# Layer 1's products as 8 bases x 16 features, with one and two picks by turns, in a two-layer graph network on one Trainium2 core

## What is computed

```python
x = _layernorm(x + L0(x, ...))
h = x
xs, y = h[src], h[dst]
c = w_comp[etype]
xb = einsum('ei,bio->ebo', xs, weight)
msg = einsum('eb,ebo->eo', c, xb)
x_hat = xs @ A1_w.T + A1_b
y_hat = y @ A2_w.T + A2_b + rel_emb[etype]
a = tanh(relu(sum(x_hat * y_hat, -1) / sqrt(32)))
nei = segment_sum(a[:, None] * msg, dst)
h_new = where(in_deg > 0, nei + h[src[last_e]] @ self_loop_weight, 0)
out = _layernorm(x + relu(h_new))
```

## Time and profile before

| | |
|---|---|
| median of 3 runs | 4324.56 us |
| profiled execution / its span | 4323.87 / 4322.1 us |
| TensorE busy, VectorE busy | 3720.5 us (86%), 2847.5 us (66%) |
| POOL busy, ACT busy | 3200.7 us (74%), 741.1 us (17%) |
| granted TensorE clock, mean over the span | 0.950 |
| DMA traffic | 649.66 MB, mean 150 GB/s |
| layer 1's first and last `x4_load` | 2215.7 and 4137.2 us |

### The profile page before, as it was taken

How to read it: one execution, slowest core, us unless ns; L and a number is a source line. 1 busy time by engine, 2 the same in 40 slices (tenths; PEclk the granted TensorE clock), 3 DMA queues, 4 the chain that set the end, 5 groups by cost and what they waited for, 6 DMA issues and landing times.

```text
span 4322.1 us, 58432 instructions
## 1 busy us (share of the span) xinstructions
PE 3720.5 (86%) x20607; PEld 1663.8 (38%) x20607; DVE 2847.5 (66%) x5125; ACT 741.1 (17%) x1303; POOL 3200.7 (74%) x3330
## 2 busy tenths in 40 slices
PE   7989999999999999941788999989999899989841
PEld 3444554554554544421333333333333333333311
DVE  8845555555555555526668888888888888888844
ACT  4411111111111111110011111111111111111111
POOL 7777777777777777767777777777777777777745
PEclk9999999999999999965899999999999999999965
DMA  8146566666666666651146666666666666666621
GB/s 340 26 109 169 148 160 148 157 160 151 156 159 152 158 156 152 159 138 33 29 104 182 176 174 168 180 174 172 170 177 175 175 171 173 176 176 169 168 60 32
DMA packets 546562, 649.66 MB, mean 150 GB/s; under 512 B 219555, under 2 KB 381888, under 8 KB 544096
## 3 DMA queue, kind: packets, MB, share of 16 engines
q1 hardware_dynamic: 394912, 480.58, 42.4%
q0 software_dynamic: 106432, 56.28, 8.3%
q10 hardware_dynamic: 44928, 109.07, 6.5%
HBM read 421.88 MB, written 223.66 MB: 149 GB/s over the span
## 4 chain that ended last, share of the span: by engine, by line
PE 54%; DMA 12%; DVE 11%; POOL 7%; issue 5%; SPq 1%; ACT 1%; DVEq 0%; POOLq 0%; ACTq 0%
PE psum L1488 23%; PE psum L1524 6%; DMA late<-xs_dram 6%; PE psum L1646 5%; DVE late L1322 5%; POOL rows_in L760 4%; DMA xs_dram<-rows_in 4%; PE psum L1573 4%; PE psum L1582 3%; PE psum L1726 3%; PE psum L1534 2%; POOL last_rows L760 2%; PE psum L1474 2%; DVE dt_ L1206 2%; DMA rows_in<-h_dram,src_idx 2%
## 5 line engine op out<-in xcount | busy, mean ns | idle before, releaser
L760 POOL DMA_INDIRECT rows_in<-h_dram,src_idx x1540 | 1453.4, 944 | 476.0 <-issue 410.0
L760 POOL DMA_INDIRECT rows_in<-in_x_dram,src_idx x1392 | 1353.6, 972 | 434.6 <-issue 418.0
L1322 DVE TENSOR_TENSOR late<-late,psum 128x512 f32<-128x512 f32 x1664 | 1082.9, 681 | 359.3 <-PE psum L1573 192.0
L1488 PE MATMUL psum<-early,late 128*128 128x448 bf16 x5712 | 1130.6, 353 | 7.1 <-DVE late L1118 5.0
L1488 PEld LDWEIGHTS psum<-early,late 128*128 128x128 bf16 x5712 | 544.8, 98 | 625.3 <-issue 137.4
L1573 PE MATMUL psum<-comp,sel 128*128 128x512 bf16 x1664 | 573.7, 385 | 168.4 <-DVE late L1322 167.1
L1582 PE MATMUL psum<-late,basis 128*32 128x512 f32 x3328 | 446.7, 609 | 0.0
L1118 DVE TENSOR_TENSOR late<-psum,lane_hot 128x448 f32<-128x448 f32 x272 | 169.9, 625 | 358.7 <-PE psum L1488 270.8
L1646 PE MATMUL psum<-x,rows_in 128*128 128x448 bf16 x1344 | 381.0, 353 | 0.0
L1573 PEld LDWEIGHTS psum<-comp,sel 128*128 128x128 bf16 x1664 | 155.5, 98 | 574.9 <-DVE late L1322 460.0
L1234 DVE TENSOR_TENSOR_SCAN scan<-fresh,scan,psum 128x512 f32<-128x512 bf16 x103 | 131.8, 1280 | 352.9 <-PE psum L1534 352.9
(11 more groups left out here) (157 smaller groups left out, 4149.8 us busy)
## 6 DMA issues: line engine op xcount, KB each, us to landing
late<-xs_dram SPq DMA_DIRECT2D x416, 256.0 KB
sp_in<-spread SPq DMA_DIRECT2D x208, 256.0 KB
late<-type_dram SPq DMA_DIRECT2D x104, 512.0 KB, 9.2
onehot_dram<-late SPq DMA_DIRECT2D x104, 512.0 KB
late<-onehot_dram SPq DMA_DIRECT2D x104, 512.0 KB
sum_rows<-early ACTq DMA_DIRECT2D x104, 512.0 KB, 2.7
spread<-late SPq DMA_DIRECT2D x16, 1664.0 KB, 40.1
ea<-in_edge_t SPq DMA_DIRECT2D x104, 256.0 KB
```

The costliest lines, as they stand in the source:

```text
L760: pool.indirect_dma_start(out=out, out_offset=None, in_=table, in_offset=bass.IndirectOffsetOnAxis(ap=index, axis=0)).then_inc(done, 16)
L1322: dve.tensor_tensor(prod[:, n % G_BUFS, :], x4[:, s.slot(2), g, :], bank[C_BANK[n]][:, :], ALU.mult).then_inc(prod_ready, 1)
L1488: last_ = pe.matmul(hot_bank[tile_slot(s, t)], class_hot[s.slot(2)][:, c, HOT - hot_tiles(s) + t, :], x_parts[:, c, q, :], start=c == 0 an ...
```

## The change

Three things change, nearly all of them in layer 1.

1. A product holds 8 bases x 16 features on its partitions, in place of 4 x 32. A coefficient tile then serves both halves of the 32 features: there are 8 coefficient tiles (2 groups of bases j, 4 streams g) and 8 double products of 128x1024, whose coefficient operand is the PSUM bank read twice (a broadcast over the two halves i). The 16 message matmuls of a step stay as they are in number and shape.
2. The source rows must now stand as 8 copies of 16 features x 2 halves: `x8` takes 2 MB a step, and `x8_load` is eight DMAs, the k-th onto partitions 16k to 16k+15, in runs of 2 KB as before.
3. `HOTS1` is (1, 2): even steps of 6 to 98 pick one tile, odd ones two (46 steps pick one tile more, so POOL issues 46 gathers fewer). The second tile uses PSUM bank 1, between the copies of `compose` and `score_sum`. `PIECES1` is written anew, and so is the order of `step1` on TensorE and VectorE. In layer 0 `hot_save` stores two tiles for the odd steps.

The diff, cut to its core (the views and index tables that only follow from the sizes are left out):

```diff
+B_GROUPS = 2
+F_GROUPS = KCH // B_GROUPS
+OPS = B_GROUPS * STREAMS
+COPIES = BASES // B_GROUPS
+FEATS = F // F_GROUPS
...
-HOTS1 = (1,)
-PIECES1 = {1: (0, 0, 6, 11, 11, 16, 21)}
+HOTS1 = (1, 2)
+PIECES1 = {1: (0, 0, 5, 12, 21), 2: (0, 7, 16, 28, 42)}
...
-C_BANK = [(2, 3, 6)[n % 3] for n in range(SLOTS - 1)] + [3]
+C_BANK = [(2, 3, 6)[n % 3] for n in range(OPS)]
...
-        hot_bank1 = [bank[5][:, 0:PICK * F]]
+        hot_bank1 = [bank[b][:, 0:PICK * F] for b in (1, 5)]
...
-                n = max(HOTS1)
+                n = max(hot1_count(s.at), 1)
...
-                wait_step(sp, s, prod_ready, each=SLOTS, lag=2)
-                for k in range(4):
-                    sp.dma_start(x4[F * k:F * k + F, u, :, :], xs_dram[u].rearrange("(g f) n -> f g n", f=F)
-                                 ).then_inc(x4_in[u], 16)
+                wait_step(sp, s, prod_ready, each=OPS, lag=2)
+                for k in range(COPIES):
+                    sp.dma_start(x8[FEATS * k:FEATS * k + FEATS, u].rearrange("p g i n -> p (g i) n"),
+                                 xs_dram[u].rearrange("(m f) n -> f m n", f=FEATS)
+                                 ).then_inc(x8_in[u], 16)
...
-                dve.tensor_tensor(prod[:, n % G_BUFS, :], x4[:, s.slot(2), g, :],
-                                  bank[C_BANK[n]][:, :], ALU.mult).then_inc(prod_ready, 1)
+                dve.tensor_tensor(prods[n], x8[:, s.slot(2), g],
+                                  bc(bank[C_BANK[n]][:, :], [P, F_GROUPS, LEN], 1), ALU.mult).then_inc(prod_ready, 1)
...
+                if hot1_count(s.at + 1) == len(hot_bank1):
+                    wait_count(pe, s, hot1_read, hot1_before(s.at + 1) + 1)
                 pe.matmul(bank[1][:, :], ones_blk[:, :], score, start=True, stop=True).then_inc(sum_done, 1)
...
-                    if rest == 0:
+                    if rest == 0 and t < hot1_count(s.at) - 1:
+                        wait_step(pe, s, comp_ready, each=2, lag=1)
+                    elif rest == 0:
                         wait_step(pe, s, query_ready, lag=1)
```

More of the change, by code:

```diff
@@ L66 @@
 CLASS_COLS = HOT_COLS + EARLY_TILES
-C_BANK = [(2, 3, 6)[n % 3] for n in range(SLOTS - 1)] + [3]
-C_FREE = [max(m for m in range(-SLOTS, n) if C_BANK[m % SLOTS] == C_BANK[n]) + 1 for n in range(SLOTS)]
-G_BUFS = 8
+C_BANK = [(2, 3, 6)[n % 3] for n in range(OPS)]
+C_FREE = [max(m for m in range(-OPS, n) if C_BANK[m % OPS] == C_BANK[n]) + 1 for n in range(OPS)]
+LATE_PRODS = 4
 BURST = 4
@@ L319, in build @@
         out1 = [out1_all[:, (u + 1) % 4] for u in range(4)]
+        y_room = early[:, NODE_COLS * F:NODE_COLS * F + 2 * F_GROUPS * LEN]
+        prods = [room[:, a:a + F_GROUPS * LEN].rearrange("p (i n) -> p i n", i=F_GROUPS)
+                 for room, n in ((late_prods, LATE_PRODS), (ea[:, :, :].rearrange("p u n -> p (u n)"), 1),
+                                 (out0[:, :, :, :].rearrange("p u k f -> p (u k f)"), 1), (y_room, 2))
+                 for a in range(0, n * F_GROUPS * LEN, F_GROUPS * LEN)]
         at[0] = 0
@@ L447, in build @@
         xs_out = [sem(f"xs_out{u}") for u in range(2)]
-        x4_in = [sem(f"x4_in{u}") for u in range(2)]
+        x8_in = [sem(f"x8_in{u}") for u in range(2)]
         hot_in = sem("hot_in")
@@ L1668, in step1 @@
                 if behind.exists():
-                    messages(behind, KCH - 1)
-                coef(s, 3)
+                    messages(behind, 2)
+                    messages(behind, 3)
                 if more:
                     compose(ahead)
-                coef(s, 4)
+                coef(s, 3)
                 if more:
@@ L1676, in step1 @@
                     spread_turn(1, ahead, 4)
-                coef(s, 5)
-                if more:
                     relate(ahead)
-                coefs(s, 6, 8)
+                coef(s, 4)
+                if pick:
+                    hot_rows(later, 0)
                 if turn:
                     source_turn(ahead)
[L1683 to L1688, removed]
+                coef(s, 5)
                 if pick:
                     hot_rows(later, 1)
-                coef(s, 11)
-                coef(s, 12)
+                messages(s, 0)
+                coef(s, 6)
+                messages(s, 1)
                 if more and not turns_last:
@@ L1698, in step1 @@
                     hot_rows(later, 2)
-                coef(s, 13)
+                coef(s, 7)
                 if pick:
                     hot_rows(later, 3)
[L1702 to L1708, removed]
                 if behind.exists():
@@ L1789 @@
         w2[o:o + HID, q, F * (g % 2):F * (g % 2) + F] = np.asarray(L0_gnn_W2)
-    sel = np.zeros((2, 64, 2, KCH, 4, F), f32)
+    sel = np.zeros((2, 64, 2, B_GROUPS, COPIES, FEATS), f32)
     for half in range(2):
         for q in range(PARTS):
-            for k in range(KCH):
-                for b in range(4):
-                    sel[half, q * BASES + 4 * k + b, half, k, b, :] = 1.0
+            for j in range(B_GROUPS):
+                for b in range(COPIES):
+                    sel[half, q * BASES + COPIES * j + b, half, j, b, :] = 1.0
     rel = np.zeros((P, F + BASES), f32)
```

67 lines of the change are left out of this document (34 added, 33 removed).

## The result

The changed kernel takes a median of 5617.98 us (5605.07 to 5641.34, 4 runs) against 4323.41 us (4322.13 to 4326.15, 4 runs): 1.3001 times as long, 95% interval 1.298 to 1.3023. Its profiled execution took 5623.68 us, of which the span is 5621.9 us. The prediction was 4637 us and its range ended at 5131; the serial load, one of its rivals, stood at 5667.

The account below looks back on a forecast made before the run. POOL's gathers were taken to bound layer 1, with the ring 2.3 us behind. A round of 16.36 + 0.15 + 5.1 = 21.6 us over 101 steps adds 302.9, other loads 10.2: 4323.9 + 313 = 4637 us, range 4265 to 5131.

Parts of the forecast that it names:

- the serial load: Rival: the eight copy DMAs go one after the other at 104 GB/s, a round of 31.6 us, 5667 us; chance 0.14.
- POOL is the bound: Layer 1 before the change: 15 gathers of 1.248 us make the 18.7 us step.
- the ring: Layer 1's loop of load, product 0, turn, store and load, once per step: 16.36 us a round before the change.
- 2.3 us of room: Layer 1: POOL's 18.67 us step less the 16.36 us loop; all that the new load may cost.
- the 57.4 us: POOL in layer 1: 46 gathers fewer at 1.248 us each, gained only while POOL is the bound.
- slower, 0.86: Whole kernel: chance of a slower time, from 0.72 for the forecast and 0.14 for the serial load.
- The load's rate: Load of the spread rows, 2.10 MB in eight DMAs: 207 GB/s assumed, 10.1 us, so +5.1 us a round.
- The path from product 0 to the turn: Layer 1, on the ring: 3.96 us before, 4.5 with two picks or 3.7 with one after, +0.15 us in the mean.
- The store's 3.9 us stay: Store of the turned source rows, on the ring: unchanged at 3.9 us.
- 21.6: Forecast length in us of one round of the ring after the change: 16.36 + 0.15 + 5.1.
- VectorE nothing, TensorE nothing: Layer 1 busy time: VectorE stays 15.2 us a step, TensorE 17.1 in the mean, below POOL's 18.1; no cost.
- hidden load: Rival: copies load at 390 GB/s, the ring is 16.8 us, POOL stays the bound, 4267 us; chance 0.11.

Follow-up runs that it names:

- e1: Changed kernel with copy k of the source rows written to every eighth partition, `sel` and `basis` permuted to match; 4766.81 us (1.1022 to the kernel before).
- e15: Changed kernel with spread copies issued by SP and ScalarE, small loads ahead of them, and the next step's source-row turn directly behind `compose`; 4332.6 us (1.0008).
- e16: e15 with the step before's two messages put back ahead of the turn, one into each of TensorE's two waits; 4277.29 us (0.989).
- e11: Changed kernel with the early turn alone: next step's source rows turned ahead of the coefficient that product 0 sets free; 5391.93 us (1.2457).
- e2: Changed kernel with SP issuing copies 0 to 3 and ScalarE copies 4 to 7, partitions still neighbouring; 5042.55 us (1.166).
- e3: Changed kernel with the edits of both e1 and e2: spread partitions and two issuing engines; 4668.73 us (1.08).

## Why the prediction was wrong

- **POOL is the bound, the ring runs close behind with 2.3 us of room, and the load decides**: right. The ring became the bound and the 57.4 us won nothing. The direction (slower, 0.86) was right.
- **The load's rate: the step that failed.** "I take the rate of the nearest row, 207 GB/s", because "if some engines get ahead and work on the next DMA, two narrow ones do together what one wide one did". They did not: 119 to 128 GB/s, and 21.7 us from first issue to product 0 (mean of 22.14 and 21.17) where 7.16 + 5.1 = 12.3 were forecast. That is +9.4 us a round. With the same bytes on every eighth partition the rate came (206 to 212 GB/s in e1), so what the step had wrong is that neighbouring 16-partition DMAs in one queue help each other along. The argument against it stood in the text, that four different old DMAs in flight had got no more than 207, and I gave the serial case only 0.14. The Trainium skill's rule ("SBUF — State Buffer", "Door 1: The DMA port swizzle": 16 neighbours reach 4 of 16 ports, 104 GB/s) would have given 5667 us, and the trace agrees with it (95 and 99 GB/s for the load, 5617.98 us). That the rival's sum came within 1% is partly luck, since it shares the two errors named next, which have opposite signs.
- **The path from product 0 to the turn**: mis-sized. 4.5 and 3.7 us forecast, 7.29 and 4.47 measured (4013.93 to 4021.22, 4047.24 to 4051.71), in the mean +1.8 us. The forecast ran this path over VectorE's product 1 and gave `spread_turn` and `relate`, which stand in TensorE's order ahead of the next coefficient, no term; in both rounds the path runs over them (1.06 + 1.40 and 0.85 + 1.40 us), and seven picks priced at 1.33 us took 2.61. The granted clock there was 0.50 and 0.51, after TensorE had sat idle for the load (12.02 us ahead of the second round). In e15's chain, where that wait is gone, the same two cost 0.44 + 0.76 us. So a longer ring here made its own TensorE part longer.
- **The store's 3.9 us stay**: 2.73 and 3.44, 0.8 us less in the mean. 21.6 + 9.4 + 1.8 - 0.8 = 32.0 us, where the two rounds have 31.9 in the mean and the 64 steps of the stretch 31.25.
- **VectorE nothing, TensorE nothing**: 1.21 us for a double product is right, and TensorE's busy time per step is no bound in the changed kernel. e15 shows that it lies close: once the load is off the chain, TensorE with two unfilled waits decides.
- **The rival "hidden load", 4267 us above 315 GB/s**: not this kernel's case. Its saving on POOL is borne out (4277 us in e16), but not its way there: e16's load still takes 12.25 us (3392.14 to 3404.39), more than the 7.16 + 1.6 that the ring had room for, and is covered because the turn has left the ring.

## What to carry to other kernels

Price a load by the partitions that each of its DMAs writes, not by its bytes alone: here several narrow DMAs in one queue added up in time, not in rate. If the layout is free, try a stride that spreads each copy over the partitions. A transfer that stands on a loop of product, turn, store and load is paid in full every step. Tuning the transfer alone won 851 us here (e1) and taking the turn out of the loop alone 226 (e11); neither was enough, and what the single queue then held back had to be moved too. Before counting a saving, read the room of the next loop: here 57 us in all stood behind a loop with 2.3 us of room a step.

## What the runs showed that I had not expected

- A stride of eight partitions in the destination raises the rate on one queue by some 70% (119 to 128 against 206 to 212 GB/s), at the same packet count and bytes (604990 packets, 778.80 MB in both). The Trainium skill's table of ports in "Door 1: The DMA port swizzle" makes that plausible: by it the partitions of such a copy lie on 8 of the 16 ports instead of 4, for which it gives 189 GB/s.
- On neighbouring partitions two issuing engines are worth more than the issue time: 5617.98 to 5042.55 us, and the load takes 17.39 and 14.74 us in e2's chain where it took 22.14 and 21.17, while its issues take 1.8 us and not 3.6. On spread ones they are not: 11.62 us in e3's chain against 14.12 in e1's, and the issues take 2.5 us less (2.5 and not 5.0). The Trainium skill says in "SBUF — State Buffer", under "Can I just issue two DMAs to hit both halves?", that two DMAs to both halves serialize (+6%) and that several issuing engines do not help. On one queue the trace agrees: the copies of the changed kernel, on different groups of partitions, do not add up (119 to 128 GB/s). With two queues it agrees on the spread copies, issue time apart, and it does not on the neighbours, where SP writes partitions 0 to 63 and ScalarE 64 to 127 (172 to 208 GB/s). The cause was not tried apart and stays open.
- A DMA share near 1 said little by itself here: 1.10, 1.05 and 1.07 stood beside 120, 206 and 326 GB/s. It has to be read with the rate.
